# A decoder layer on one core: the stacked rows of q and k, stored and loaded with two pairs of heads side by side

## The reference, cut to what matters

```
q, k, v = x@Wq+bq, x@Wk+bk, x@Wv+bv          # 16 heads of 16 channels
scores  = einsum('bhqd,bhkd->bhqk', q, k) / sqrt(16), -10000 above the diagonal
probs   = softmax(scores);  ctx = einsum('bhqk,bhkd->bhqd', probs, v)
x = layernorm(x + ctx@Wo + bo)
... cross-attention, layernorm, router, top 2 of 8 experts, layernorm
```

## Time and profile before

| | us |
|---|---|
| runs of the kernel before: median | 692.32 |
| lowest, highest of 3 | 691.11, 706.74 |
| the profiled execution, its own time | 693.73 |
| its span in the trace | 692.0 |
| PE busy | 603.4 (87%) |
| DVE busy | 530.1 (77%) |
| ACT, POOL busy | 407.9 (59%), 303.2 (44%) |
| DMA: moved, mean rate | 103.65 MB, 150 GB/s |

### The profile page before, as it was taken

The page is one execution under the profiler, slowest core; times in us unless marked ns, Lnnn a source line. Parts: engine busy times, 40 slices in busy tenths (PEclk is TensorE's granted clock), DMA queues, the critical chain, the costliest instruction groups (busy, mean ns, idle before and its releaser), DMA issues. The chain is left out here.

```text
span 692.0 us, 13570 instructions
## 1 busy us (share of the span) xinstructions
PE 603.4 (87%) x5232; PEld 414.6 (60%) x5232; DVE 530.1 (77%) x930; ACT 407.9 (59%) x622; POOL 303.2 (44%) x363
## 2 busy tenths in 40 slices
PE   5989688887999799898987853899999999999984
PEld 2435344453444535454654543698989989988963
DVE  4687576528877688877757779699999999999725
ACT  3655578763466344455651313388888988987613
POOL 9311255545356244625452434325464642662223
PEclk9999999999999999999999995699999999999998
DMA  7407454394002900111020017578888779786264
GB/s 229 143 1 176 100 153 153 104 254 163 1 1 92 218 28 14 48 64 31 1 94 30 0 35 239 169 260 267 300 288 283 264 267 290 264 279 208 92 227 161
DMA packets 70992, 103.65 MB, mean 150 GB/s; under 512 B 4848, under 2 KB 56776, under 8 KB 69904
## 3 DMA queue, kind: packets, MB, share of 16 engines
q1 hardware_dynamic: 67184, 92.55, 42.3%
q0 software_dynamic: 3744, 10.23, 4.2%
HBM read 80.28 MB, written 22.41 MB: 148 GB/s over the span
## 5 line engine op out<-in xcount | busy, mean ns | idle before, releaser
L240 DVE TENSOR_REDUCE rowmax<-M 128x1 f32<-128x512 f32 (+3 forms) x176 | 104.6, 636 | 37.6 <-PE M L230 35.5
L681 ACT ACTIVATE probs<-R 128x1024 f32<-128x1024 f32 x80 | 80.4, 1028 | 51.2 <-PE R L1035 50.9
L213 PE MATMUL HB<-xT,w 128*128 128x256 f16 (+1 forms) x1104 | 107.8, 258 | 0.3 <-DVE xT L1615 0.3
L1770 PE MATMUL YB<-w,h 128*128 128x256 f16 x936 | 105.9, 273 | 0.1
L213 PEld LDWEIGHTS HB<-xT,w 128*128 128x128 f16 x1104 | 94.8, 98 | 11.2 <-DVE xT L1615 1.7
L1770 PEld LDWEIGHTS YB<-w,h 128*128 128x128 f16 x936 | 91.4, 98 | 10.8 <-issue 0.4
L543 POOL TENSOR_SCALAR_AFFINE_SELECT probs<-probs 128x256 f32<-128x256 f32 x128 | 49.6, 407 | 97.4 <-ACT probs L681 96.9
L1467 ACT ACTIVATE hf<-HB,b 128x256 f32<-128x256 f32 (+1 forms) x184 | 69.9, 445 | 37.0 <-PE HB L213 35.5
L1388 POOL DMA_INDIRECT scratch_ys<-y,dst x39 | 41.9, 1075 | 98.2 <-ACT y L1447 93.0
L1380 POOL DMA_INDIRECT xg<-scratch_xs,src x39 | 62.4, 1601 | 26.6 <-issue 10.9
L1642 DVE SCALAR_TENSOR_TENSOR h<-hf,h 128x512 f16<-128x512 f32 (+1 forms) x92 | 56.6, 616 | 3.2
(11 more groups left out here) (272 smaller groups left out, 1071.7 us busy)
## 6 DMA issues: line engine op xcount, KB each, us to landing
w1f<-in_W SPq DMA_DIRECT2D x23, 1024.0 KB, 7.6
w2f<-in_W SPq DMA_DIRECT2D x23, 1024.0 KB, 6.0
scratch_qk<-qk SPq DMA_DIRECT2D x18, 256.0 KB, 3.0
scratch_ax<-stage SPq DMA_DIRECT2D x16, 256.0 KB, 2.5
scratch_vw<-stage SPq DMA_DIRECT2D x16, 256.0 KB, 2.9
vw<-scratch_vw SPq DMA_DIRECT2D x4, 1024.0 KB, 7.4
a_x<-scratch_ax SPq DMA_DIRECT2D x4, 1024.0 KB, 9.5
parts<-scratch_ys SPq DMA_DIRECT2D x8, 512.0 KB, 8.6
```

The source lines that it names most:

```text
L213: last = nc.tensor.matmul(out, left(a, k), right(b, k), start=(k == 0 and m == 0), stop=(k == n - 1 and m == 2))
L240: return nc.vector.tensor_reduce(rowmax[:, t, par * PAIRS + p0:par * PAIRS + p0 + pairs], bank[:, 0:pairs * wide].rearrange("p (n w) -> p ...
L681: A.activation(probs[:, n % RING, :, :], bank[:, :, :], ACT.Exp, scale=1.0 / (QS * QS)).then_inc(empty, 1)
L1770: last = M.matmul(YB[q][:, t, :], h[:, q, a, m, t * 128:t * 128 + 128], w2[:, q, b, m, :], start=((m, a, b) == (0, 0, 0)), stop=((m, a) == ...
```

## The change

The row of DRAM is numbered (t, p, m, c) instead of (t, c, p, m): the two blocks of channels of one channel p and place m lie side by side, 2 KB together. A store writes both blocks of a partition as one line. The high part stands in two of the three places, so it is stored to both by one DMA that reads its source twice (`to_broadcast`), and the low part by another: four stores, of 512 and 256 KB, instead of six. A load takes lines of 2 KB, four for each partition, into two neighbouring places of the tile. So place 2q + c of the tile now holds pair 4c + q of the model: `place_of` gives the place of a pair, the score step reads it there, and the stamp of batch 0 fills the places in that order. The maxima and their copy run over places as before. `places` is also used by `kinds_of`, with the same result as before.

```diff
-STORES, LOADS = 6, 4
+STORES, LOADS = 4, 4
...
+def places(x, hl):
+    at = [m for m in range(3) if PARTS[x][m] == hl]
+    return slice(at[0], at[-1] + 1, at[-1] - at[0] or 1), len(at)
...
+    def place_of(pair):
+        return pair % (PAIRS // DC) * DC + pair // (PAIRS // DC)
...
             elif kind == "store":
                 sp.wait_ge(qlo_done, 2 * b + 2)
-                rows = dram["qk"][b * 6 * D:(b + 1) * 6 * D, :].rearrange("(t c p m) s -> t m p c s", t=2, c=DC, m=3)
-                for t, parts in enumerate(PARTS):
-                    for m, hl in enumerate(parts):
-                        sp.dma_start(rows[t, m, :, :, :], qk[:, hl, 2 * t:2 * t + 2, :]).then_inc(qk_stored, 16)
+                rows = dram["qk"][b * 6 * D:(b + 1) * 6 * D, :].rearrange("(t p m c) s -> t p m (c s)", t=2, m=3, c=DC)
+                for t in range(2):
+                    for hl in range(2):
+                        where, many = places(t, hl)
+                        sp.dma_start(rows[t, :, where, :], flat(qk[:, hl, 2 * t:2 * t + 2, :]).unsqueeze(1)
+                                     .to_broadcast([128, many, DC * S])).then_inc(qk_stored, 16)
...
-                rows = dram["qk"][b * 6 * D:(b + 1) * 6 * D, :].rearrange("(t p r e) s -> t r e p s", t=2, r=2, e=STACK)
+                rows = dram["qk"][b * 6 * D:(b + 1) * 6 * D, :].rearrange(
+                    "(t q r e c) s -> t r e q (c s)", t=2, r=2, e=STACK, c=DC)
                 for t, dst in enumerate((qs[b % 2], ks[b % 2])):
                     for par in range(2):
-                        sp.dma_start(dst[64 * par:64 * par + STACK, :, :], rows[t, par, :, :, :]).then_inc(stack_in[b % 2], 16)
+                        sp.dma_start(dst[64 * par:64 * par + STACK, :, :].rearrange("e (q c) s -> e q (c s)", c=DC),
+                                     rows[t, par, :, :, :]).then_inc(stack_in[b % 2], 16)
...
-                rows = slice(32 * (n % 4), 32 * (n % 4) + 32)
+                rows, c = slice(32 * (n // DC), 32 * (n // DC) + 32), n % DC
                 for x in range(2):
                     for hl in range(2):
-                        last = M.matmul(bank[:, x, :], stamp[rows, x, hl, :], qk[rows, hl, 2 * x + n // 4, :],
+                        last = M.matmul(bank[:, x, :], stamp[rows, x, hl, :], qk[rows, hl, 2 * x + c, :],
...
-                    p = 2 * (n // ITEMS) + x
+                    p = place_of(2 * (n // ITEMS) + x)
```

More of the change, by code:

```diff
@@ L346, in kinds_of @@
     def kinds_of(x, hl):
-        at = [m for m in range(3) if PARTS[x][m] == hl]
-        step = at[1] - at[0] if len(at) > 1 else 1
+        where, many = places(x, hl)
         return stamp[:, x, hl, :].rearrange("p (r e) -> p r e", r=2)[:, :, 0:STACK].rearrange(
-            "p r (d m) -> p r d m", m=3)[:, :, :, at[0]:at[-1] + 1:step], len(at)
+            "p r (d m) -> p r d m", m=3)[:, :, :, where], many
     def fold_done(eng):
```

## The result

| | changed | before, beside it |
|---|---|---|
| median, us | 701.18 | 699.53 |
| runs, us | 699.97, 701.18, 702.1, 701.19 | 692.32, 691.11, 706.74, 707.48 |
| profiled execution, its span | 699.97, 698.2 | 693.73, 692.0 |
| mean granted clock of that execution | 0.955 | 0.969 |

The ratio is 1.0136, 95% interval 1.0105 to 1.0166. The comparison leaves out executions more than 1.5% above the fastest of their kernel, so on the side of before only 692.32 and 691.11 stand in it; the medians of all four runs a side are 1.65 us apart. Forecast were 691.1 us and a range of 685.0 to 695.5: the measured median lies outside, on the slow side. The difference is under 2%, but a loss of 9 us against those two runs needed an explanation.

A forecast was written before the change was run, and what follows sets the result against it. TensorE, busy 87% of the span, was taken to wait twice for stack loads; gains of 0.4 (issue) and 0.4 + 0.4 (loads), 1.2 us, took the median from 692.32 to 691.1 us, range 685.0 to 695.5.

The forecast's parts named there:

- What bounds the kernel, and where the change acts: Attention stage: TensorE waits twice for stack loads, in batches 2 and 3, 6.5 us together; both waits stay, 5 to 6 us.
- Issue term: SyncE in batch 2: fewer store issues let the VW store and the loads leave 0.4 us sooner; batches 1 and 3, 0.
- Load term: Stack loads in batches 2 and 3: 2 KB lines make them 5% quicker, 0.4 us in each batch.
- the core of the argument: Stack loads are slow because they land on 48 partitions, which isn't changed; the line's share is 0 to 1.0 us per round.
- Rival A: Stack loads: the line is the limit, so both waits go; 6.5 us gained, 685.8 us; chance 0.16.
- rival C: Packets stay at 1 KB because the dimensions don't merge; only two stores' issue is saved, 691.9 us; chance 0.07.
- Rival B: Stack loads in batches 2 and 3 slow to 143 GB/s; 5.0 us more, 697.3 us; chance 0.11.
- The sign that the prediction set for B: Landings of the stack loads over 2.3 us apart would show rival B; about 2.1 us was forecast.
- The pauses: TensorE's waits for the last load before m:2:0 and m:3:0: about 2.2 and 3.5 us would remain.
- The sum, 1.2 us: Whole kernel: 0.4 us from issue in batch 2 plus 0.4 and 0.4 us from loads in batches 2 and 3.
- the clock falls as before in batch 3: TensorE's granted clock falls to 0.50 after the pause in batch 3, as in the kernel before.

The follow-up runs named there:

- held back: Either kernel with GpSimd's large memsets waiting for VectorE's four stamp casts: the kernel before 697.99 us, ratio 0.9988; the changed kernel 699.01 us, ratio 1.0004.
- The load probe: The kernel before plus five groups of four 384 KB loads into an idle tile, varying line length and partitions; 714.79 us, not compared because of the added work.
- The kernel with the lines alone: The changed kernel with six stores of 256 KB instead of four, keeping 2 KB lines and the new pair order; 698.63 us, ratio 0.9988.
- The changed kernel held back and filled: The changed kernel with GpSimd's memsets waiting for the stamp casts, and constant matmuls ahead of VW:0:0, m:2:0 and m:3:0; 696.28 us, ratio 0.9996.
- the one filled: The kernel before with matmuls on constants in two pauses, 10 ahead of m:2:0 and 13 ahead of m:3:0; 702.71 us, ratio 1.0018.

## Why the prediction was right or wrong

**What bounds the kernel, and where the change acts**: right. Two waits of PE on the ks loads, a pause left in both batches; together 6.3 us, a little over the forecast 5 to 6, and 6.7 to 7.4 in the other profiles of the changed kernel with unfilled pauses. The packets under 2 KB are fewer by 9312 (forecast 9216). The stores cost 0.71 us each to issue instead of 0.64, the two with the repeated source included, so 2.83 us instead of the forecast 2.6.

**Issue term, 0.4 us in batch 2**: the step from stores to VW issue came true to the tenth (7.90 to 7.49 us). The step from there to the loads was taken as unchanged and is 0.44 us longer, in every profile. The term is 0.0.

**Load term, 0.4 us in each of two batches**: from load issue to m:2:0, 11.95 us in the mean of six profiles with 1 KB lines and unfilled pauses, 11.41 in seven of the changed kernel (each with one held back among them): 0.5 us. In batch 3 12.58 and 12.54: nothing. So 0.5 instead of 0.8. The load probe, where 2 KB lines land no faster than 1 KB lines, speaks against the rate of a load as the cause of it. The kernel with the lines alone has 11.55 us too, in one profile, so it isn't the merged stores; what it is isn't shown. That slowness is by place, the core of the argument, is shown. Rival A (the line is the limit) and rival C (the lines don't merge) are out. Rival B is out as well: the landings of batch 2 are 2.2 us apart as before ((158.0 - 151.5) / 3), those of batch 3 2.4 us, before 2.6. (The sign that the prediction set for B, over 2.3 us, was no sign: batch 3 had it before the change.)

**The pauses**: 2.89 and 3.42 us for 2.2 and 3.5. The second was hit by luck: in the six other profiles of the changed kernel with unfilled pauses it is 3.80 to 4.24 us, no shorter than the 3.78 to 4.32 of the kernel before. For batch 2 the prediction reckoned the pause as if only its end moved. The same VW store whose landing it had moved with the loads also releases ctxT, and with it the o steps ahead of the pause, so its start moved by more than its end.

**The sum, 1.2 us**: at the same clock the changed kernel is 0.41 ± 0.56 us faster, which fits the measured 0.0 + 0.5 + 0.0 and doesn't exclude nothing at all.

**What failed is the step from the sum to the time.** The prediction said that the sum "is 693.73 us around a span of 692.0; it becomes 692.5", that the median of before is 692.32, and that "the runs before differ by that much without any change", by which it meant 1 us. The third run of before, 706.74, stood in the table and was passed over. The kernel's runs have a standard deviation of 4.8 us and a mean of 698.15; 692.32 was a median of three with two near the low end. Even the three runs shown said so: their mean is 696.7 and their standard deviation 8.7, so by these the forecast would have stood near 695.5, with a range of 8 us or more to each side, and 701.18 in it. The prediction also held the clock fixed ("the clock falls as before in batch 3"), where the mean granted clock of the kernel before goes from 0.943 to 0.972 in its 93 runs, worth 16 us at 5.7 us for each 0.01.

So the first 9 us come from two low runs of before; the 6 us between the two profiles are falls of the clock, about half of the lost clock where no store or load of the stack runs; and over 60 and 93 runs no such difference is there. What stays open: whether a small loss of up to 2 us by more falls is real (+0.84 ± 1.40 us; the clock lower by 0.0022 ± 0.0023); why the clock falls in one execution and not in another; what the 0.5 us from load to m:2:0 are; and what SyncE does in its 0.44 us.

No version here beats both kernels for certain. The changed kernel held back and filled has the lowest median of its set, 696.28 us, but its mean is only 1.4 ± 2.3 us below the mean of the 93 runs of before.

## What to carry to other kernels

Before lengthening the lines of a slow transfer, compare its rate with a transfer of the same lines that lands on all partitions: if that one is clearly faster (here landings 1.3 us apart against 2.1 to 2.4), the lines aren't what is slow. Forecast a change from the spread of runs, not from one profile and a median of three: if three runs lie 15 us apart, a gain of 1 us can't be read from four. And when two profiles differ, compare the granted clock by stage first; where the stretches that differ hold the same instructions at another clock, look at a second profile of the same kernel before looking for a cause.

## What the runs showed of the hardware

- The granted clock of one and the same stretch fell or didn't from execution to execution: around the store issue of batch 2 to 0.79 over 8 us in one of the last three profiles of the kernel before and not in the other two. The pair at 139.25 us, one of each kernel, shows it with the busy times and the clock before it alike. Each 0.01 of mean clock goes with 5.7 us.
- Loads of 393 KB on 48 partitions landed 2.3, 2.4 and 2.1 us apart with lines of 1, 2 and 8 KB, that is at 164 to 190 GB/s; on 128 partitions with 1 KB lines 1.3 us apart.
- Four small casts by VectorE at the start take 0.48 us if GpSimd's memsets wait for them, 5.24 us beside them in 15 of 17 profiles, and 17.35 us in the other two; then the first q matmul starts at 20.46 us instead of 9.86, and these two executions stood some 11 us above the line of time against clock. The start of the kernel before held back, and of the one filled, which had the late start (timelines):

```profile
2.85 0.48 DVE L745 CAST stamp<-squares 128x64 f16<-128x64 f32 x4
3.39 1.81 POOL L507 MEMSET v_aug<- 128x2048 f32 x1 [0.65 <-DVE stamp L745]
```

```profile
2.85 17.35 DVE L744 CAST stamp<-squares 128x64 f16<-128x64 f32 x4
...
13.08 7.07 POOL L511 MEMSET v_diag<- 128x4096 f16 x2
...
20.46 1.86 PE L213 MATMUL R<-xT,w_hl 128*128 128x512 f16 x4 [13.59 <-DVE w_hl L756]
```

The casts end with the last memset at 20.2 us. The Trainium skill, SBUF — State Buffer, section "🔬 SBUF: two separate sides", says that VectorE in one of its modes and GpSimd lock a shared pair of ports for a whole instruction and block each other; these rows fit that, though they don't show VectorE's mode, and holding GpSimd back took the wait away. It won no time, since the first q matmul started at 9.85 us all the same; whether it keeps the late start away stays open, as no run of that set stood so far above the line.
